# First cross attention of a perceiver block: head 0's stacks built in place instead of moved by transfers

## The reference, cut to what matters

```python
def _L0_xattn_ref(qkv, y):              # qkv: the normed x, 256 x 512; y: the context, 4096 x 512
    N_HEADS = 16
    bs, width, length = qkv.shape       # 1, 256, 512
    ch = width // N_HEADS               # 16 channels
    q = qkv.reshape(bs * N_HEADS, ch, length)
    k = v = y.reshape(bs * N_HEADS, ch, -1)           # 16 heads x 16 channels x 8192 keys
    scale = 1.0 / math.sqrt(math.sqrt(ch))
    weight = jnp.einsum('bct,bcs->bts', q * scale, k * scale)
    weight = jax.nn.softmax(weight.astype(jnp.float32), axis=-1)
    a = jnp.einsum('bts,bcs->bct', weight, v)
```

## Time and profile before

| | us |
|---|---|
| median of 3 runs (lowest to highest) | 1435.17 (1434.88 to 1435.29) |
| the profiled execution, its own time | 1436.34 |
| its span | 1434.6 |
| PE busy in it | 1375.6 (96%) |
| DVE busy | 1151.8 (80%) |
| ACT busy | 940.2 (66%) |
| POOL busy | 138.4 (10%) |

### The profile page before, as it was taken

The page is one execution under the profiler, slowest core; times in us unless marked ns, Lnnn a source line. Parts: engine busy times, 40 slices in busy tenths (PEclk is TensorE's granted clock), DMA queues, the critical chain, the costliest instruction groups (busy, mean ns, idle before and its releaser), DMA issues. The chain is left out here.

```text
span 1434.6 us, 27306 instructions
## 1 busy us (share of the span) xinstructions
PE 1375.6 (96%) x10680; PEld 837.0 (58%) x10680; DVE 1151.8 (80%) x1670; ACT 940.2 (66%) x1764; POOL 138.4 (10%) x171
## 2 busy tenths in 40 slices
PE   3999999999999999999899899999989889999998
PEld 2433333333333333333458899999978664567997
DVE  5999999999999999997486666666658456887665
ACT  1588888888888888888184545555434540785453
POOL 4122221221122222110000000000000000000000
PEclk9999999999999999999999999999999999999999
DMA  7544665555454455544205555544446514203651
GB/s 179 145 106 105 161 137 119 141 146 125 110 118 114 96 124 111 95 69 68 88 1 219 207 183 195 193 176 175 176 157 269 235 66 169 67 2 111 183 187 38
DMA packets 63281, 192.54 MB, mean 134 GB/s; under 512 B 32840, under 2 KB 33264, under 8 KB 51248
## 3 DMA queue, kind: packets, MB, share of 16 engines
q1 hardware_dynamic: 62976, 190.80, 46.4%
q10 hardware_dynamic: 192, 0.20, 0.1%
HBM read 165.72 MB, written 21.83 MB: 131 GB/s over the span
## 5 line engine op out<-in xcount | busy, mean ns | idle before, releaser
L530 DVE TENSOR_REDUCE pm<-bank 128x1 f32<-128x1024 f32 x512 | 621.3, 1221 | 14.9 <-PE bank L611 9.3
L589 ACT ACTIVATE probs<-bank 128x512 f32<-128x512 f32 x1024 | 554.5, 598 | 97.7 <-PE bank L630 92.2
L611 PE MATMUL bank<-kst,qst 48*128 48x512 f32 x1024 | 371.1, 452 | 21.9 <-DMA qst<-qsplit 20.1
L630 PE MATMUL bank<-qst,kst 52*128 52x512 f32 (+1 forms) x1024 | 372.4, 448 | 1.5 <-DVE pm L530 0.8
L647 PE MATMUL bank<-probs,vext 128*32 128x256 f32 x3968 | 316.7, 391 | 0.0
L630 PEld LDWEIGHTS bank<-qst,kst 52*128 52x128 f32 (+1 forms) x1024 | 153.0, 185 | 210.9 <-ACT probs L589 182.0
L1373 PE MATMUL bank<-e_xhi,e_hi 128*128 128x256 f32 (+1 forms) x768 | 219.4, 286 | 4.5 <-DVE e_lo L1308 3.9
L1373 PE MATMUL bank<-e_xlo,e_hi 128*128 128x256 f32 (+1 forms) x768 | 219.0, 285 | 0.0
L1373 PE MATMUL bank<-e_xhi,e_lo 128*128 128x256 f32 (+1 forms) x768 | 219.0, 285 | 0.0
L647 PEld LDWEIGHTS bank<-probs,vext 128*32 128x32 f32 x3968 | 78.1, 108 | 181.2 <-ACT probs L589 91.3
L611 PEld LDWEIGHTS bank<-kst,qst 48*128 48x128 f32 x1024 | 149.8, 186 | 29.4 <-DMA qst<-qsplit 20.1
(11 more groups left out here) (220 smaller groups left out, 1516.5 us busy)
## 6 DMA issues: line engine op xcount, KB each, us to landing
raw<-wall SPq DMA_DIRECT2D x43, 1536.0 KB, 6.5
kst<-kscratch SPq DMA_DIRECT2D x192, 128.0 KB, 4.5
kscratch<-ksplit SPq DMA_DIRECT2D x15, 1024.0 KB, 4.7
kraw<-ctx_rows SPq DMA_DIRECT2D x16, 512.0 KB, 6.3
vraw<-ctx_vt SPq DMA_DIRECT2D x16, 512.0 KB, 7.1
ctxT<-ctxT SPq DMA_DIRECT2D x8, 1024.0 KB, 11.9
nat<-ctx_chunks SPq DMA_DIRECT2D x6, 1024.0 KB, 22.1
weights<-wscratch SPq DMA_DIRECT2D x16, 256.0 KB, 3.5
```

What stands on the lines that cost most here:

```text
L530: nc.vector.tensor_reduce(pm[:, h % 2, r % 4, c:c + 1], bank[:, 2 * (r % 2):2 * (r % 2) + 2, :], AX.XY, ALU.max).then_inc(pre_reduced, 1)
L589: nc.scalar.activation(probs[:, (XST * k + n) % PR, :], bank[:, S_BANK[k][n], :], ACT.Exp, scale=XSCALE).then_inc(probs_ready, 1)
L611: ins = nc.tensor.matmul(bank[:, 2 * (r % 2) + j, :], qst[64 * j:64 * j + KR, h, tt * P:tt * P + P], kst[64 * j:64 * j + KR, h % 2, c * 51 ...
L630: nc.tensor.matmul(bank[:, S_BANK[k][n], :], kst[64 * j:64 * j + rows, h % 2, m * P:m * P + P], qst[64 * j:64 * j + rows, h, :], start=Tru ...
```

## The change

Head 0 no longer goes through the split, DRAM and the stacking transfers for its queries and its first key half:

- SP first loads `xstack` (x's 16 rows of head 0, eight times over 128 partitions), then `X`, then `krep`: the 2048 keys of both j, each repeated four times over 64 partitions, in two column parts (512, 1536). The source of these transfers has the repeat count (8, and 4) as its outermost dimension. Then `kraw` 0 and 1 and `vraw` 0.
- DVE derives 0/1 columns `is_rest` and +1/-1 columns `sign` from `ident`. It norms `xstack` alone (`xnstack`), with statistics of `X` and `xstack` together, and makes `qst` of head 0 as normed x times `is_rest` plus or minus the rounded high part.
- ACT does the same for the keys in four chunks of 512 columns (`khigh`, and `krep` times `is_rest` in place); POOL adds the two into `kst[:, 0, :]`. The ACT square root stands behind chunk 0.
- POOL memsets `marks` first. After its four additions it does `split(0)`, then the norm of `X` and the query split that DVE did, then `split(1)`.
- SP issues the `marks` transfers when all four additions are done, then `store_split(0)` in one piece, waits for its landing, then `load_stack(0, 1)`, then the loop. `load_q(1)` waits for POOL's query split.
- PE does 8 matmuls of `ident` (128 columns) when the square root is done, before `pre(0, 0)`, and waits for each 512 columns of keys in turn.

```diff
@@ -45 +45 @@
 DLAG = 3
+FIRST_COLS = 512
+FIRST_WARM = 8
@@ -243 +245 @@
     marks = at(0, "marks", [4, 2, XK // 2], F32R)
+    krep = at(16, "krep", [P, XK // 2])
+    khigh = at(24, "khigh", [P, XK // 2], F32R)
+    xstack = at(96, "xstack", [P, D])
+    xnstack = at(98, "xnstack", [P, D])
+    qhigh = at(100, "qhigh", [P, D], F32R)
+    fstats = at(102, "fstats", [P, 3, 6])
+    fmv = at(102.125, "fmv", [P, 3, 2])
+    fvar = at(102.25, "fvar", [P, 3, 1])
+    fstd = at(102.375, "fstd", [P, 3, 1])
+    frstd = at(102.5, "frstd", [P, 3, 1])
+    is_rest = at(102.625, "is_rest", [P, 2])
+    sign = at(102.75, "sign", [P, 2])
     nscratch = nc.dram_tensor("nscratch", [XN, P, 32], F32, kind="Internal").ap()
@@ -252 +266 @@
     split_stored = sem("split_stored")
-    first_high_stored = sem("first_high_stored")
+    first_keys = sem("first_keys")
     stack_lo = [sem("stack_lo0"), sem("stack_lo1")]
...
     v_ready = sem("v_ready")
-    qsplit_ready = sem("qsplit_ready")
+    queries_ready = sem("queries_ready")
     pre_scores = sem("pre_scores")
@@ -282 +296 @@
...
+    signs = []
     with nc.Block() as block:
@@ -298 +313 @@
             def store_split(h):
-                sp.wait_ge(split_step, 2 * h + 2)
+                sp.wait_ge(split_step, 4 + 2 * h + 2)
                 sp.dma_start(kscratch[h].rearrange("k p n -> p k n"), ksplit[:, :, :].bitcast(F32)).then_inc(split_stored, 16)
@@ -346 +361 @@
+            sp.dma_start(xstack[:, :], x[0:XC].unsqueeze(0).to_broadcast([P // XC, XC, D])).then_inc(x_loaded, 16)
             sp.dma_start(X[:, :, :], x.rearrange("(a p) d -> p a d", p=P)).then_inc(x_loaded, 16)
+            keys = ctx_rows[0].rearrange("(c s) n -> c (s n)", c=XC)
+            for lo, hi, moved in ((0, FIRST_COLS, stack_lo[0]), (FIRST_COLS, XK // 2, stack_lo[1])):
+                for j in range(2):
+                    sp.dma_start(krep[64 * j:64 * j + 64, lo:hi],
+                                 keys[:, j * XK + lo:j * XK + hi].unsqueeze(0).to_broadcast([4, XC, hi - lo])).then_inc(moved, 16)
             load_raw(0)
             load_raw(1)
-            sp.wait_ge(split_step, 1)
-            sp.dma_start(kscratch[0, 0], ksplit[:, 0, :].bitcast(F32)).then_inc(first_high_stored, 16)
-            sp.wait_ge(split_step, 2)
-            sp.dma_start(kscratch[0, 1], ksplit[:, 1, :].bitcast(F32)).then_inc(split_stored, 16)
-            sp.wait_ge(first_high_stored, 16)
-            load_rows(0, 0, K_ROWS[0])
-            load_rows(0, 0, K_ROWS[2])
+            load_v(0)
+            sp.wait_ge(const_set, 2)
+            sp.wait_ge(first_keys, 4)
+            for b in range(2):
+                for j in range(2):
+                    row = 64 * j + KR
+                    sp.dma_start(kst[row:row + 4, b, :].bitcast(F32),
+                                 marks[:, :, :].rearrange("k s n -> k (s n)").bitcast(F32)).then_inc(negmax_stacked, 16)
+            store_split(0)
             sp.wait_ge(split_stored, 16)
-            load_rows(0, 0, K_ROWS[1])
-            sp.wait_ge(stack_lo[0], 192)
             load_stack(0, 1)
-            sp.wait_ge(qsplit_ready, 4)
@@ -368 +388 @@
                     store_split(h + 1)
-                if h == 0:
-                    load_v(0)
-                    sp.wait_ge(const_set, 2)
-                    for b in range(2):
-                        for j in range(2):
-                            row = 64 * j + KR
-                            sp.dma_start(kst[row:row + 4, b, :].bitcast(F32),
-                                         marks[:, :, :].rearrange("k s n -> k (s n)").bitcast(F32)).then_inc(negmax_stacked, 16)
                 if h < XH - 1:
                     load_stack(h + 1, 0)
+                    if h == 0:
+                        sp.wait_ge(queries_ready, 1 + 2 * TA)
                     load_q(h + 1)
@@ -401 +415 @@
                 if h < XH - 3:
-                    sp.wait_ge(split_step, 2 * h + 4)
+                    sp.wait_ge(split_step, 4 + 2 * h + 4)
                     load_raw(h + 3)
@@ -434 +448 @@
                     pool.wait_ge(split_stored, 16 * h)
-                    if h == 1:
-                        pool.wait_ge(first_high_stored, 16)
                     nc.gpsimd.tensor_copy(ksplit[:, 0, :], kraw[:, h % 2, :]).then_inc(split_step, 1)
-                pool.wait_ge(split_step, 2 * h + 1)
+                pool.wait_ge(split_step, 4 + 2 * h + 1)
                 nc.gpsimd.tensor_tensor(ksplit[:, 1, :], kraw[:, h % 2, :], ksplit[:, 0, :].bitcast(F32),
@@ -447 +459 @@
-            split(0)
-            pool.wait_ge(qsplit_ready, 4)
-            split(1)
             nc.gpsimd.memset(marks[:, :, :].bitcast(F32), 1.0).then_inc(const_set, 1)
...
             nc.gpsimd.memset(marks[0:2, 1, :].bitcast(F32), 0.0).then_inc(const_set, 1)
+            for c in range(4):
+                cols = slice(512 * c, 512 * c + 512)
+                pool.wait_ge(split_step, c + 1)
+                nc.gpsimd.tensor_tensor(kst[:, 0, cols], krep[:, cols], khigh[:, cols].bitcast(F32), ALU.add).then_inc(first_keys, 1)
+            split(0)
+            pool.wait_ge(queries_ready, 1)
+            for a in range(TA):
+                nc.gpsimd.tensor_scalar(xn[:, a, :], X[:, a, :], fmv[:, a, 0:1], frstd[:, a, :],
+                                        ALU.subtract, ALU.mult).then_inc(g.xn_ready, 1)
+                pool.wait_ge(g.xn_ready, a + 1)
+                nc.gpsimd.tensor_copy(qsplit[:, 0, a], xn[:, a, :]).then_inc(queries_ready, 1)
+                pool.wait_ge(queries_ready, 2 * a + 2)
+                nc.gpsimd.tensor_tensor(qsplit[:, 1, a], xn[:, a, :], qsplit[:, 0, a].bitcast(F32), ALU.subtract).then_inc(queries_ready, 1)
+            split(1)
             nc.gpsimd.tensor_copy(g.identb[:, :], ident[:, :]).then_inc(g.ident_ready, 1)
@@ -507 +530 @@
-            dve.wait_ge(x_loaded, 16)
-            norm_dve(g, dve, 0, link)
-            for a in range(TA):
-                dve.wait_ge(g.xn_ready, a + 1)
-                nc.vector.tensor_copy(qsplit[:, 0, a], xn[:, a, :]).then_inc(qsplit_ready, 1)
-                dve.wait_ge(qsplit_ready, 2 * a + 1)
-                nc.vector.tensor_tensor(qsplit[:, 1, a], xn[:, a, :], qsplit[:, 0, a].bitcast(F32), ALU.subtract).then_inc(qsplit_ready, 1)
+            dve.wait_ge(g.ident_ready, 2)
+            groups = ident[:, :].rearrange("p (j g c) -> p g j c", j=2, g=4)
+            for n in range(2):
+                ins = nc.vector.tensor_reduce(is_rest[:, n:n + 1], groups[:, 1 + n], AX.XY, ALU.add)
+            link(ins)
+            link(nc.vector.tensor_scalar(sign[:, :], is_rest[:, :], -2.0, 1.0, ALU.mult, ALU.add))
+            signs.append(dve_step.n)
+            dve.wait_ge(x_loaded, 32)
+            rows = [X[:, 0, :], X[:, 1, :], xstack[:, :]]
+            for a in range(3):
+                ins = nc.vector.bn_stats(fstats[:, a, :], rows[a])
+            link(ins)
+            for a in range(3):
+                ins = nc.vector.bn_aggr(fmv[:, a, :], fstats[:, a, :])
+            link(ins)
+            nc.vector.tensor_scalar(fvar[:, :, :], fmv[:, :, 1:2], EPS, None, ALU.add).then_inc(g.var_ready, 1)
+            dve.wait_ge(g.std_ready, 1)
+            link(nc.vector.reciprocal(frstd[:, :, :], fstd[:, :, :]))
+            link(nc.vector.tensor_tensor(fstd[:, :, :], frstd[:, :, :], frstd[:, :, :], ALU.mult))
+            link(nc.vector.scalar_tensor_tensor(out=fstd[:, :, :], in0=fstd[:, :, :], scalar=-0.5, in1=fvar[:, :, :],
+                                                op0=ALU.mult, op1=ALU.mult))
+            link(nc.vector.scalar_tensor_tensor(out=frstd[:, :, :], in0=fstd[:, :, :], scalar=1.5, in1=frstd[:, :, :],
+                                                op0=ALU.add, op1=ALU.mult))
+            link(nc.vector.tensor_scalar(xnstack[:, :], xstack[:, :], fmv[:, 2, 0:1], frstd[:, 2, :], ALU.subtract, ALU.mult))
+            link(nc.vector.tensor_scalar(qhigh[:, :], xnstack[:, :], sign[:, 1:2], None, ALU.mult))
+            nc.vector.scalar_tensor_tensor(out=qst[:, 0, :], in0=xnstack[:, :], scalar=is_rest[:, 1:2], in1=qhigh[:, :].bitcast(F32),
+                                           op0=ALU.mult, op1=ALU.add).then_inc(queries_ready, 1)
@@ -572 +615 @@
...
             nc.scalar.activation(g.warm[:, :], ident[:, 0:1], ACT.Sqrt)
+            act.wait_ge(dve_step.sem, signs[0])
+            for c in range(4):
+                cols = slice(512 * c, 512 * c + 512)
+                if c < 2:
+                    act.wait_ge(stack_lo[c], 32)
+                nc.scalar.activation(khigh[:, cols], krep[:, cols], ACT.Copy, scale=sign[:, 0:1])
+                nc.scalar.activation(krep[:, cols], krep[:, cols], ACT.Copy, scale=is_rest[:, 0:1]).then_inc(split_step, 1)
+                if c == 0:
+                    act.wait_ge(g.var_ready, 1)
+                    nc.scalar.activation(fstd[:, :, :], fvar[:, :, :], ACT.Sqrt).then_inc(g.std_ready, 1)
             act.wait_ge(kraw_loaded[0], 16)
```

(21 more changed lines are left out.)

## The result

| | before | after |
|---|---|---|
| median of 4 runs each on one chip (lowest to highest) | 1435.03 (1434.43 to 1435.29) | 1461.01 (1457.77 to 1472.82) |
| ratio, 95% interval | | 1.0192 (1.0159 to 1.0224) |
| the profiled execution, its own time | 1436.34 | 1472.82 |
| its span | 1434.6 | 1471.0 |

The kernel got slower, as forecast, but by 26 us where 7.7 were forecast, and its 1461.01 lies above 1447, the upper end. The runs of after also lie 15 us apart, those of before 1. The profiled execution of after is its slowest; its account (+36.48) is made against before's profiled one.

The account below looks back on a forecast made before the run. Busy PE from 80 to 640 us passes on any shift of the first score, which SP's chain sets: +5.8 for the later score and +1.9 for PE's clock give +7.7, 1435.17 to 1442.9, range 1433.5 to 1447.

Parts of the forecast that it names:

- half of 3.8 is lost: 1.9: PE behind the first score: after some 5 us idle, 3.8 us of work at half clock costs 1.9, bounds 0 and 2.7.
- the score's shift: First score moves from 47.72 to 53.5 through SP's chain: 5.8 us later.
- Four engines: Key loads: a source with 4 outermost pieces uses 4 DMA engines, at 25.7 GB/s each.
- the rest at 16.25: SP's chain: the rest of the keys behind chunk 0 (8.6) lands at 16.25 us.
- PE's first matmul: PE and DVE's chain: queries ready at about 13, first matmul at 12 to 14 us.
- Last addition 21.3: POOL's last key addition, 1.28 long behind ACT's copies at 20.0, ends at 21.3 us.
- Marks: issue 3.24: SP's queue: marks take 3.24 to issue, to 24.5; store_split(0) queues behind their data and lands at 33.3.
- The later legs: SP's queue from load_stack(0,1) to the score: 9.46, then 2.75, 3.73 and 4.32 us, score at 53.5.
- POOL's norm of x: POOL's norm of x and query split: 4.6 to 6.2 us, ending by 30 and covered.
- Marks free: Rival: four engines, but marks hold nothing up; store lands at 29.2, score at 49.5, total 1438.9; chance 0.11.
- spread: Rival: repeats spread over all 16 engines; keys land at 8.0, SP's chain at 45.6, total 1435.0; chance 0.13.
- Slow keys: Rival: four engines at the pace of marks, 33 GB/s; keys take 31.8 instead of 10.2, total 1464.5; chance 0.03.

Follow-up runs that it names:

- e8: Kernel after plus 104 keep-busy matmuls ahead of pre(1, 0) and 48 ahead of the first score, leaving no PE idle ahead of the score: 1454.34, ratio 1.0123.
- e11: e10 with the eight krep transfers of partitions 64 to 127 issued by ACT instead of SP: 1435.05, ratio 0.9997 against before.
- e5: Kernel after with the raw loads (kraw 0 and 1, vraw 0) held until krep has landed: 1457.09, one run.
- e4: Kernel after with marks cut in eight pieces, six of them issued before the wait for POOL's additions: 1455.03, one run.
- e10: Kernel after with e1 and e4, POOL's small memsets right behind the marks' and stack_negmax(0) ahead of all head 1 transfers: 1435.69, ratio 1.0010 against before.
- e1: Kernel after with krep loaded by 16 transfers of 16 partitions instead of 4 with outermost count 4: 1453.2, ratio 1.0113 against before.
- e2: Kernel after with krep's source taken from heads 0 to 3 instead of head 0 four times (output differs): 1453.9, one run.

## Why the prediction was right and wrong, point by point

**Direction, and what bounds: right.** SP's chain set the score, PE was idle ahead of it (4.13; some 5 forecast), and the shift reached the end one for one (e8: 17.3 of shift, 17.75 of time). For a score earlier than before's that did not hold: e11's 2.78 had shrunk to 0.56 at 666 us.

**The step that failed most in the profiled execution: "half of 3.8 is lost: 1.9".** It measured 20.2 there (0.5 in e8). I took the length of the low stretch from one other place, a stage of other matmuls (3.0 us of work there, by the clock of its windows, not 3.8), and gave it a bound of 2.7, as if one row could bound it. Across the kernels here it lasted 14 to 50 us. Of the 28.8 that the profiled pair lies over the forecast of +7.7, this term is 18.3; the other 10.5 are the score's shift, 5.8 forecast and 16.25 measured: 6.7 by the keys, 2.9 by marks and store, 0.7 by `stack_negmax`, as told below. By the medians it is the other way round. Of the 18.3 between 26.0 and 7.7, the shift is again 10.5, if it was the same in the other runs, and the clock 7.8 (9.7 against 1.9). Either one alone takes the median past 1447.

**Four engines: right, as far as the share of 0.25 shows it; "the rest at 16.25": 22.88.** The pace per engine was 22 GB/s and not 25.7, and loads issued behind it slowed it (e5). Chunk 0 came at 12.16 instead of 8.6, `xstack` and `X` at 7.0 instead of 6.0. PE's first matmul was at 17.35, not 13: chunk 0, plus 1.04 for a 128x3 DVE operation beside POOL's addition, which I had put at 0.2.

**Last addition 21.3: 28.0**, for the rest of the keys (+6.6).

**Marks: issue 3.24, store landed 12.0 behind the last addition: 5.62 and 14.9.** The mechanism, the store behind marks' data, was right (9.1 from issue to landing; e4 gives 5.3). The size of the issue was not: SP stood still longer than in before, and the store's own issue took 2.49 instead of about 0.4. Why is not shown.

**The later legs: right.** 9.46 from `load_stack(0,1)` to the landing of `store_split(1)`: 9.57 (42.89 to 52.46). `load_stack(1,0)` 2.75: 2.63. `load_q(1)`: 3.73. `stack_negmax` to score 4.32: 5.05. `pre(1,0)` was forecast as covered, at 39 to 48: it waited until 50.27, but ended ahead of the score all the same.

**POOL's norm of x: 8.2, bounds 4.6 to 6.2.** Its tensor_scalar took 2.07 each, over the dear end of 1.3, which was DVE's. It was covered in after, since `split(1)` waits for the landing at 42.9; e4 shows that it is the next to be late once marks are away.

**Rivals.** "Marks free" and "spread" are refuted by the 9.1 and the 0.25. "Slow keys" (4 engines at marks' pace, 1464.5) came nearest in time, for another reason. What no rival had was a price that grows behind the score.

## What to carry to other kernels

Before a PE-bound stretch, ask not only how late it starts but whether PE is idle just ahead of it: here a wait of 4 us cost 20 more at the low clock in one execution and some 6 to 12 in the others, and filler matmuls that kept PE busy to the last moment took most of this back (the median fell from 1461.0 to 1454.3) without starting the work any sooner. Look at the outermost count of a transfer's source: 4 meant a quarter of the DMA share here. And a price at which only one row stands, from a stage of other instructions, has no known upper bound: keep the range open on that side. Last, once the first wait is repaired, follow the gain through the stage: the next waits can use it up.

## What the runs showed of the hardware

- Behind an idle of 2.6 to 10 us ahead of the first score the granted clock stayed at 0.50 for 14 to 50 us although PE was busy throughout; behind a like idle of 3.43 at 681.8 it was back after 3.0 us of work (the window 688 to 689 has 0.90), and behind the 9.20 ahead of `pre(1, 0)` in after after 5.9.
- The clock need not fall inside the wait: in after it was 1.00 from 62 to 63, PE idle, and 0.55 from 63 to 64, where the score starts; in e10, behind an idle of 2.38, it was 1.00 for the first 1.9 us of work and then 0.50 for 3.4.
- A transfer whose source has an outermost count of 4 used a share of 0.25, with repeated rows or not; with 64 rows at one stride the share was 1.03.
- A full share does not fix the rate: from 3 to 8 us e1 moved 234 GB/s at 1.01 and e2, without repeated key rows, 248 at 1.03; the first loads of before moved 411 at 1.04.
- A POOL tensor_scalar of 128x512 with two columns as operands took 2.07 us, a POOL addition or subtraction of the same size 1.25 to 1.29, DVE's tensor_scalar 0.55 beside an idle POOL.
